# Graph transformer on one core: a chunk's first row gather waits for the landing of the chunk before

## The chip, the cores and the metric

One core of one Trainium2 chip runs the whole program. The metric is device time in microseconds (us) of one execution, from the first to the last instruction; lower is better. Time before: median 3657.33 us of 3 runs (3653.97 to 3659.31).

The engines are TensorE (PE; its weight load is PEld), VectorE (DVE), ScalarE (ACT), GpSimd (POOL) and SyncE (SP). Each has its own instruction queue and works through it in order. They tell each other by semaphores: an instruction or a DMA adds to one when it is done, another engine waits until it has reached a number.

## The reference, cut to what matters

Two layers of graph attention over N = 6250 nodes with D = 128 features, H = 8 heads, and E = 200000 directed edges that come sorted by their target (`dst`), then a feed-forward part for each node and a last layer norm:

```
loops = jnp.arange(n); src = concatenate([edge_index[0], loops]); dst = concatenate([edge_index[1], loops])
for l in range(L):                                   # L = 2
    xn = _layernorm(x, ln1_g[l], ln1_b[l])
    xp = xn + xn @ Wpos[l] + bpos[l] + deg[:, None] * Wdeg[l][0] + bdeg[l]
    q, k, v = (xp @ W[l] + b[l]).reshape(n, H, HD)   # one for each of Wq, Wk, Wv
    att = clip(einsum('ehd,ehd->eh', q[dst], k[src]) / scale, -50, 50)
    alpha = softmax of att over the edges of one dst
    aggr = segment_sum(v[src] * alpha[:, :, None], dst)
    x = x + (aggr @ Wo[l] + bo[l])
    x = x + gelu(_layernorm(x, ln2_g[l], ln2_b[l]) @ W1[l] + b1[l]) @ W2[l] + b2[l]
```

The expensive part is `k[src]` and `v[src]`: for each edge, one row of 256 f32 (1 KiB) out of a table in HBM, at a place that the data decide.

## The kernel before, in words

**Tables.** Before each layer the kernel has written `kv_table[l]` (a row of keys and values for each node) and `q_table[l]` to HBM. For layer 1 the node steps of layer 0 write them, tile by tile of 128 nodes (L780, L781).

**Units.** The edges of a layer are worked off in units. Most are *chunks* of CH = 1024 edges (T = 8 tiles of P = 128 edges). The edges of the last 8 (layer 0) or 10 (layer 1) node tiles are done as *blocks* instead: they are sorted by source on the chip, whole stretches of `kv_table` are loaded by SP (L729), and TensorE picks the rows by one-hot matmuls (L952) that ACT copies out (L1238). `Layer.unit_order` mixes the two: 165 chunks and 56 blocks in layer 0, 157 chunks and 70 blocks in layer 1, so 322 chunks and 126 blocks in all.

**What a chunk goes through.** POOL gathers its rows (`gather`, L1961): eight indirect DMAs, one for each tile of 128 edges, each moving 128 rows of 1 KiB into the chunk's buffer. TensorE spreads the queries to the edges (`spread_chunk`, L993), DVE multiplies them with the gathered keys (`make_products`, L1676, which waits at L1671 until all eight gathers have landed) and reduces them to scores (L1685), ACT makes the exponentials (L1260), DVE multiplies them with the gathered values (`make_messages`, L1700, which adds 1 to `msg_ready`), TensorE sums over the edges of a node (L1009), DVE adds that to the running sums (L1726). The steps for whole nodes (projection, feed-forward, next layer's tables) are put between the units by a table of slots.

**Buffers and semaphores of the gathers.** The gathered rows have a ring of RING_KV = 4 buffers, `kv[m % 4]`: three in the tile `kv_ring`, the fourth in the tile `arena`. Each buffer has a semaphore `gathered[m % 4]`, to which each of the chunk's eight gathers adds 16 when its rows have landed, 128 for a chunk. POOL's queue in this stage (`pool_edges`, L1975) holds nothing but the gathers of all chunks in order. The first gather of chunk m waits until `msg_ready` says that chunk m - 4 has been read out of the same buffer (L1963, L1964); chunk m = 3 waits for tables of the setup instead (L1965 to L1969); the first chunk of each layer waits for the layer's `kv_table` (L1978). POOL does not wait for its own gathers to land.

The seven lines that matter, of `gather`:

```
m = chunk(l, c)
if m >= RING_KV:
    e.wait_ge(msg_ready, chunk_unit(m - RING_KV) + 1)
...
for t in range(T):
    e.indirect_dma_start(kv[m % RING_KV][:, t, :], None, kv_table[l],
                         bass.IndirectOffsetOnAxis(ap=src_idx[:, c * T + t:c * T + t + 1], axis=0)
                         ).then_inc(gathered[m % RING_KV], 16)
```

Of the kernel before, what the change touches and what calls it, by code (L numbers as in the profile page):

```python
# [30 lines left out]
T = 8  # L31
# [21 lines left out]
RING_KV = 4  # L53
# [237 lines left out]
def graph_transformer(nc, x, src, dst, Wq, bq, Wk, bk, Wv, bv, Wo, bo, Wpos, bpos, Wdeg, bdeg,  # L291
                      ln1_g, ln1_b, ln2_g, ln2_b, W1, b1, W2, b2, out):
    with ExitStack() as ctx:
# [3 lines left out]
        def semaphore(name):  # L297
            return ctx.enter_context(nc.semaphore(name))
# [227 lines left out]
        gathered = [semaphore(f"gathered{i}") for i in range(RING_KV)]  # L526
# [80 lines left out]
        def chunk(l, c):  # L607
            return LAYERS[l].chunk0 + c
# [9 lines left out]
        def chunk_unit(m):  # L618

            l = max(l for l in range(L) if LAYERS[l].chunk0 <= m)  # L620
            return unit(l, LAYERS[l].chunk_at[m - LAYERS[l].chunk0])
# [74 lines left out]
        def wait_tables(e, l, of):  # L696

            if l == 0:
                for queue in range(2):
                    e.wait_ge(tables_out[2 * of + queue], 16 * len([g for g in groups if g[0] % 2 == queue]))  # L700
            else:
                for s in range(WORK):
                    e.wait_ge((kv_out, q_out)[of][s], 16 * layer_uses(s))
# [1256 lines left out]

        def gather(e, l, c):  # L1961
            m = chunk(l, c)
            if m >= RING_KV:  # L1963
                e.wait_ge(msg_ready, chunk_unit(m - RING_KV) + 1)  # L1964
            elif m == RING_KV - 1:  # L1965

                wait_tables(e, 0, 1)
                e.wait_ge(zero_out, 16 * L)
                e.wait_ge(win_out, 16)  # L1969
# [5 lines that stand above are left out]
        def pool_edges(e):  # L1975
            e.wait_ge(idx_ready, 4)
            for l in range(L):
                wait_tables(e, l, 0)  # L1978
                for c in range(LAYERS[l].ca):
                    gather(e, l, c)  # L1980
# [206 lines left out]
```

## Time and profile before

| what | value |
|---|---|
| median of 3 runs | 3657.33 us (3653.97 to 3659.31) |
| span of the profiled execution | 5559.9 us |
| POOL busy | 2472.4 us, 44% of that span |
| DVE busy | 2916.7 us, 52% |
| PE busy | 3461.6 us, 62% |
| ACT busy | 1771.1 us, 32% |
| DMA | 548.28 MB, mean 99 GB/s; of this 337.81 MB by POOL's gathers |

The profiled execution took 5559.9 us, which is 1.52 times the median of the runs that were timed: with the profiler recording, this program runs much longer. Durations of instructions come from that execution; its idle times belong to it alone. Busy time counts an engine's instructions; its waits, and the instructions with which it issues DMAs, are not in it, but a gather on POOL shows as an instruction of its own (DMA_INDIRECT), which ends before its data have moved.

### The profile page before, as it was taken

To read this page: it belongs to the slowest core of one execution; us is meant where nothing else is said; L and a number is where in the kernel's file an instruction comes from. 1 tells how busy PE (TensorE), PEld (TensorE's weight loads), DVE (VectorE), ACT (ScalarE), POOL (GpSimd) and SP (SyncE) were. 2 spreads that over 40 slices of the span, in tenths; PEclk is the share of its full clock that TensorE was granted. 3 is DMA by queue.
4 is the path that set the end of the run, shared out by engine and by line. 5 is a ranking of instruction groups with operands and counts; after the bars stand their busy time and mean duration, and the time that the engine had idled before them with its cause. 6 is when DMAs were issued, how large, how long until landed. Compare 5 with 4: busy or idle time off the path is not lost.

```text
span 5559.9 us, 72300 instructions
## 1 busy us (share of the span) xinstructions
PE 3461.6 (62%) x24196; PEld 2666.6 (48%) x24475; DVE 2916.7 (52%) x6780; ACT 1771.1 (32%) x4391; POOL 2472.4 (44%) x2597
## 2 busy tenths in 40 slices
PE   5834656655665656666566376666666566666666
PEld 4623445444454445444444254455555455545545
DVE  9944545554454545555455354554554454545455
ACT  2301232323333332323234133333333333333334
POOL 1065444444444444444542544445444454444443
PEclk7756777777777777777777677777777777777777
DMA  2133333333333333333332333333333333333332
GB/s 73 49 111 87 88 106 93 102 88 95 102 94 99 94 102 89 104 95 96 107 105 65 106 103 109 108 107 113 96 108 106 108 110 113 111 102 115 109 104 73
DMA packets 404556, 548.28 MB, mean 99 GB/s; under 512 B 78348, under 2 KB 318656, under 8 KB 403988
## 3 DMA queue, kind: packets, MB, share of 16 engines
q0 software_dynamic: 123648, 337.81, 20.9%
q1 hardware_dynamic: 273030, 198.56, 11.9%
q10 hardware_dynamic: 7506, 7.20, 0.4%
q8 instruction: 203, 3.33, 0.2%
q14 instruction: 169, 1.38, 0.1%
HBM read 518.00 MB, written 25.29 MB: 98 GB/s over the span
## 4 chain that ended last, share of the span: by engine, by line
PE 32%; another core or an unknown queue 30%; DVE 14%; issue 12%; ACT 10%; DVEq 0%; SPq 0%; DMA 0%; ACTq 0%
PE psum L952 7%; PE psum L993 4%; PE psum L1009 3%; ACT scratch L1227 3%; PE psum L1042 3%; PE psum L1026 3%; DVE att L1685 2%; PE psum L970 2%; ACT arena L1238 2%; DVE scratch L1676 2%; DVE kv_ring L1394 1%; PE psum L1123 1%; DVE work L1377 1%; DVE scratch L1700 1%
## 5 line engine op out<-in xcount | busy, mean ns | idle before, releaser
L1971 POOL DMA_INDIRECT kv_ring<-kv_table,src_idx x1936 | 1846.4, 954 | 2132.8 <-DVE scratch L1700 1501.1
L1227 ACT ACTIVATE scratch<-psum 128x512 f32<-128x512 f32 x1148 | 649.5, 570 | 2061.3 <-remote 1442.0
L952 PE MATMUL psum<-arena 128*128 128x256 f32 x1764 | 631.5, 486 | 464.2 <-issue 194.2
L1971 POOL DMA_INDIRECT arena<-kv_table,src_idx x640 | 607.8, 950 | 664.6 <-DVE scratch L1700 489.7
L1726 DVE SCALAR_TENSOR_TENSOR arena<-psum,in_block,arena 128x136 f32 x644 | 200.9, 353 | 1286.4 <-remote 1187.3
L993 PE MATMUL psum<-q_win,scratch 64*128 64x128 f32 x5152 | 534.3, 349 | 285.7 <-issue 149.9
L952 PEld LDWEIGHTS psum<-arena 128*128 128x128 f32 x1764 | 372.6, 236 | 621.0 <-issue 319.2
L1009 PE MATMUL psum<-scratch 128*64 128x136 f32 x5152 | 519.1, 330 | 185.4 <-issue 154.2
L993 PEld LDWEIGHTS psum<-q_win,scratch 64*128 64x128 f32 x5152 | 443.2, 243 | 343.1 <-issue 332.5
L1238 ACT COPY arena<-psum 128x512 f32<-128x512 f32 x504 | 265.1, 532 | 986.9 <-remote 524.7
L1685 DVE TENSOR_REDUCE att<-scratch 128x64 f32<-128x1024 f32 (+1 forms) x448 | 525.1, 1172 | 0.1
L1676 DVE TENSOR_TENSOR scratch<-psum,arena 128x512 f32<-128x512 f32 (+1 forms) x412 | 255.4, 646 | 507.4 <-remote 397.5
L1009 PEld LDWEIGHTS psum<-scratch 128*64 128x64 f32 x5152 | 376.8, 161 | 268.6 <-issue 245.6
L1676 DVE TENSOR_TENSOR scratch<-psum,kv_ring 128x512 f32<-128x512 f32 x484 | 313.7, 684 | 264.5 <-remote 182.6
L1026 PE MATMUL psum<-q_win,scratch 128*128 128x128 f32 x1764 | 272.1, 318 | 288.4 <-ACT arena L1238 270.5
L1042 PE MATMUL psum<-scratch 128*128 128x136 f32 x1764 | 309.2, 332 | 3.8 <-ACT work L1326 3.8
L1700 DVE TENSOR_TENSOR scratch<-kv_ring,psum 128x1024 f32<-128x1024 f32 x242 | 292.3, 1208 | 29.4 <-ACT psum L1260 24.2
L1042 PEld LDWEIGHTS psum<-scratch 128*128 128x128 f32 x1764 | 289.6, 238 | 8.6 <-issue 4.5
L1026 PEld LDWEIGHTS psum<-q_win,scratch 128*128 128x128 f32 x1764 | 273.4, 234 | 12.7 <-issue 3.9
L962 PEld LDWEIGHTS psum<-plan_mem,places 128*128 128x128 bf16 x322 | 35.9, 112 | 423.5 <-issue 372.6
L1700 DVE TENSOR_TENSOR scratch<-arena,psum 128x896 f32<-128x896 f32 (+1 forms) x206 | 232.1, 1127 | 9.0 <-ACT psum L1260 7.4
L1731 DVE TENSOR_TENSOR arena<-arena,psum 128x136 f32<-128x136 f32 x108 | 31.9, 295 | 330.6 <-PE psum L1042 200.0
(251 smaller groups left out, 4873.9 us busy)
## 6 DMA issues: line engine op xcount, KB each, us to landing
arena<-kv_table SPq DMA_DIRECT2D x126, 896.0 KB
kv_ring<-kv_table,src_idx POOLq DMA_INDIRECT x1936
q_win<-q_table SPq DMA_DIRECT2D x644, 32.0 KB
work<-kv_table SPq DMA_DIRECT2D x98, 128.0 KB
arena<-kv_table,src_idx POOLq DMA_INDIRECT x640
q_win<-q_table SPq DMA_DIRECT2D x126, 64.0 KB
work<-q_table SPq DMA_DIRECT2D x98, 64.0 KB
kv_table<-work SPq DMA_DIRECT2D x49, 128.0 KB
```

Of the source, the lines that this page charges most:

```text
L952: mm = e.matmul(to[:, t % 2 * 2 * D:(t % 2 + 1) * 2 * D], hot_source[:, t * P:(t + 1) * P], source_rows[:, t, :], start=True, stop=True)
L993: m = e.matmul(q_edge[h][:, t * P:(t + 1) * P], hotT[n % 2][h * HALF:(h + 1) * HALF, t * P:(t + 1) * P], q_win[h * HALF:(h + 1) * HALF, n ...
L1009: m = e.matmul(to[h * HALF:(h + 1) * HALF], by_edge[:, t * P + h * HALF:t * P + (h + 1) * HALF], msg[n % 2][:, h * T // 2 + t, :], start=t ...
L1026: m = e.matmul(q_edge[f % 2][:, (t - ts[0]) * P:(t - ts[0] + 1) * P], hotT[n % 2][:, t * P:(t + 1) * P], q_win[:, n % 2, :], start=True, s ...
L1042: m = e.matmul(edge_sum(l, u), hot[n % 2][:, t, :], msg[n % 2][:, t, :], start=t == 0, stop=t == last)
L1227: e.activation(to[:, at:at + width], apart[k % 2][:, 0:width], ACT.Relu, bias=1.0, scale=-1.0).then_inc(apart_read, 1)
L1238: e.copy(kv_block[:, ts[0]:ts[-1] + 1, :].rearrange("p t d -> p (t d)"), apart[k % 2][:, 0:len(ts) * 2 * D]).then_inc(apart_read, 1)
L1676: e.tensor_tensor(prod[:, ts[0] * P:(ts[-1] + 1) * P].rearrange("p (t d) -> p t d", d=D), q_edge[f % 2][:, 0:len(ts) * P].rearrange("p (t ...
L1685: e.tensor_reduce(raw_att.rearrange("p t h -> p (t h)"), prod[:, 0:ts * P].rearrange("p (g d) -> p g d", d=HD), AX_X, ALU.add).then_inc(sc ...
L1700: e.tensor_tensor(msg[n % 2][:, 0:ts, 0:D].rearrange("p t (h d) -> p t h d", d=HD), values.rearrange("p t (h d) -> p t h d", d=HD), ex[:, ...
L1726: e.scalar_tensor_tensor(out=row, in0=of_edges, scalar=in_block[:, k, i:i + 1], in1=row, op0=ALU.mult, op1=ALU.add).then_inc(acc_added, 1)
L1971: e.indirect_dma_start(kv[m % RING_KV][:, t, :], None, kv_table[l], bass.IndirectOffsetOnAxis(ap=src_idx[:, c * T + t:c * T + t + 1], axis ...
```

## The change

Before the first gather of each chunk but the very first, POOL waits until the eight gathers of the chunk before have landed in full: until `gathered` of that chunk's buffer has reached 128 times the number of times that the buffer has been filled. The wait stands ahead of the one for `msg_ready`. Nothing else is changed.

```
         def gather(e, l, c):
             m = chunk(l, c)
+            if m >= 1:
+                e.wait_ge(gathered[(m - 1) % RING_KV], 16 * T * ((m - 1) // RING_KV + 1))
             if m >= RING_KV:
                 e.wait_ge(msg_ready, chunk_unit(m - RING_KV) + 1)
             elif m == RING_KV - 1:
```

## Rows read from the trace of the kernel before

**Rows 1.** The page: the span, and each engine's busy time, share and instructions.

```profile
span 5559.9 us, 72300 instructions
PE 3461.6 (62%) x24196; PEld 2666.6 (48%) x24475; DVE 2916.7 (52%) x6780; ACT 1771.1 (32%) x4391; POOL 2472.4 (44%) x2597
```

**Rows 2.** Windows: setup, gathers of layer 0, gathers of layer 1, the end.

```profile
core 0: us, PE busy (x) PEld busy (x) DVE busy (x) ACT busy (x) POOL busy (x), PEclk, DMA share, GB/s
0.00:278.00 278.00, 199.68 (x2136) 152.45 (x2136) 255.89 (x445) 75.85 (x160) 18.15 (x21) 0.75 0.20 61
278.00:3053.00 2775.00, 1647.39 (x11152) 1269.17 (x11286) 1403.84 (x3326) 827.90 (x2080) 1265.14 (x1320) 0.73 0.33 96
3053.00:5503.00 2450.00, 1578.78 (x10678) 1216.53 (x10823) 1223.83 (x2902) 839.72 (x2087) 1189.12 (x1256) 0.76 0.36 108
```

**Rows 3.** Groups of POOL's gathers, by buffer: count, busy us, mean ns of one.

```profile
L1971 POOL DMA_INDIRECT kv_ring<-kv_table,src_idx x1936 | 1846.4, 954 | 2132.8 <-DVE scratch L1700 1501.1 <-issue 534.0 <-DMA kv_table<-work 70.3
L1971 POOL DMA_INDIRECT arena<-kv_table,src_idx x640 | 607.8, 950 | 664.6 <-DVE scratch L1700 489.7 <-issue 174.9
```

**Rows 4.** POOL's waits: us in total, times, longest us.

```profile
POOL kv_ring L1971 <- DVE scratch L1700: 1501.1, 198, 17.9
POOL kv_ring L1971 <- issue: 534.0, 1736, 1.2
POOL arena L1971 <- DVE scratch L1700: 489.7, 66, 20.5
POOL arena L1971 <- issue: 174.9, 574, 0.3
POOL kv_ring L1971 <- DMA kv_table<-work: 70.3, 1, 70.3
```

**Rows 5.** Timeline of POOL: two chunks' gathers without a wait, then a waiting one.

```profile
2012.76 0.94 POOL L1971 DMA_INDIRECT kv_ring<-kv_table,src_idx  x1 [14.54 <-DVE scratch L1700]
2014.01 0.94 POOL L1971 DMA_INDIRECT kv_ring<-kv_table,src_idx  x1 [0.30 <-issue]
...
2031.51 0.95 POOL L1971 DMA_INDIRECT kv_ring<-kv_table,src_idx  x1 [0.30 <-issue]
2042.85 0.94 POOL L1971 DMA_INDIRECT arena<-kv_table,src_idx  x1 [10.39 <-DVE scratch L1700]
```

**Rows 6.** Timeline of POOL: the first and the last gather of the program.

```profile
278.64 9.23 POOL L1971 DMA_INDIRECT kv_ring<-kv_table,src_idx  x1 [27.59 <-DMA kv_table<-scratch]
...
5501.81 0.95 POOL L1971 DMA_INDIRECT kv_ring<-kv_table,src_idx  x1 [0.30 <-issue]
```

**Rows 7.** Timeline where layer 1 begins: its first chunk's gathers, queries and product.

```profile
3053.18 0.94 POOL L1971 DMA_INDIRECT kv_ring<-kv_table,src_idx  x1 [70.25 <-DMA kv_table<-work]
...
3057.65 2.08 PE L993 MATMUL psum<-q_win,scratch 64*128 64x128 f32 x16 [3.53 <-issue]
...
3061.93 0.95 POOL L1971 DMA_INDIRECT kv_ring<-kv_table,src_idx  x1 [0.30 <-issue]
...
3064.83 1.29 DVE L1676 TENSOR_TENSOR scratch<-psum,kv_ring 128x512 f32<-128x512 f32 x2 [14.30 <-issue]
```

**Rows 8.** The gathers' line: who waited for it (us, times).

```profile
  DVE scratch L1676: 14.3, 1
```

**Rows 9.** Windows behind the gather of 2031.51; the last two columns are DMA.

```profile
2033.00:2033.50 0.50, 0.00 (x0) 0.00 (x0) 0.00 (x0) 0.00 (x0) 0.00 (x0) 0.50 0.67 156
2033.50:2034.00 0.50, 0.00 (x0) 0.00 (x0) 0.00 (x0) 0.00 (x0) 0.00 (x0) 0.50 0.28 107
2034.00:2034.50 0.50, 0.00 (x0) 0.00 (x0) 0.00 (x0) 0.00 (x0) 0.00 (x0) 0.50 0.00 0
```

**Rows 10.** DMA issues of other queues, KB each, median us to landing.

```profile
q_table<-scratch SPq DMA_DIRECT2D x1, 384.0 KB, 2.8
q_table<-arena SPq DMA_DIRECT2D x3, 384.0 KB, 3.3
kv_table<-arena SPq DMA_DIRECT2D x3, 768.0 KB, 3.9
```

More of the change, by code:

```diff
@@ L1962, in gather @@
             m = chunk(l, c)
+            if m >= 1:
+                e.wait_ge(gathered[(m - 1) % RING_KV], 16 * T * ((m - 1) // RING_KV + 1))
             if m >= RING_KV:
```

## The prediction

> **What bounds the kernel now.** The first thing to read is the span against the times. The profiled execution took 5559.9 us [rows 1], the timed runs 3657.3 us in the median. So 1902.6 us of what the profile shows as idle do not exist in the timed runs, and a share of the span (POOL 44%) says little about them. The idle times of this profile can't be used as slack. What can be used is work: an engine whose work, laid end to end, comes near to 3657 us has no slack in the timed runs, whatever the profile shows around it.
>
> So I next read the engines' work per stage [rows 2]. From 278 to 5503 us PE is busy 1647.4 + 1578.8 = 3226.2 us, DVE 2627.7 us, ACT 1667.6 us, POOL 2454.2 us. With the 278.6 us before the first gather and the 57.1 us behind the last one (which ends at 5501.81 + 0.95 = 5502.76, [rows 6]; 5559.9 - 5502.8) PE would come to 3561.9 us, and that at a granted clock of 0.73 to 0.76, with more to gain where it is higher. DVE comes to 2963.4 us.
>
> POOL's busy time leaves something out. In the timeline of POOL [rows 5] a gather lasts 0.94 to 0.95 us, but the next one begins 1.25 us after its begin: from 2012.76 to 2031.51 there are 15 steps of 1.25 us with 0.30 us between two gathers, and nothing ends that gap but the queue's own issue. The waits [rows 4] show the total: 1736 + 574 = 2310 such gaps, 534.0 + 174.9 = 708.9 us. The other 264 gathers were held by `msg_ready`. Had they not been, each would still have had its 0.30 us, 79.2 us. POOL's path is then, with the busy time of [rows 3]:
>
> 278.6 (before the first gather) + 2454.2 (1846.4 + 607.8, 2576 gathers) + 708.9 + 79.2 + 70.3 (the wait for layer 1's table, [rows 4]) + 57.1 (after the last gather) = 3648.3 us.
>
> That is 99.8% of the median of 3657.3 us. I read it so: in the timed runs POOL issues gathers nearly without pause, and the ring of four buffers is mostly waiting to be filled. In the profiled execution it is the other way round: there POOL waits 1501.1 + 489.7 = 1990.8 us for DVE to free a buffer [rows 4].
>
> A page of the Trainium skill bears on the choice of 1.25 over 0.95 us. "Perfetto Trace Analysis", section "Per-instruction lifecycle: what the profiler-reported window actually captures", says of GpSimd that the reported span of an instruction is unreliable and that one should take the spacing from start to start. By the durations alone POOL's path would be 2454.2 + 406.0 = 2860.2 us and far from the bound. By the spacing it is the bound. The equal steps in [rows 5] agree with the page.
>
> **The change part by part.** It adds one wait ahead of each chunk but the first, 321 of 322. It removes and moves nothing. Behind the waiting gather in POOL's queue stand only the gathers of this and the later chunks; SP's queue, with the loads of queries, plans and source rows, is not touched. Who waits for POOL is DVE, at L1671.
>
> What one wait costs. Up to now the first gather of a chunk could start 0.30 us after the last one of the chunk before. Now it starts when that one has landed. The profile lists no landing for POOL's gathers, but it has one place where something waited for them alone: the begin of layer 1 [rows 7]. The eighth gather of the first chunk begins at 3061.93 and ends at 3062.88; the queries had been spread by 3059.73; DVE's product begins at 3064.83, and the line's own view names it as the one that waited for a gather [rows 8]. From the end of the last gather to the start of the waiting engine: 1.95 us, and 2.90 us from its begin. In place of 0.30 us this costs 1.65 us for a chunk.
>
> Bounds for that. Below: behind the gather that begins at 2031.51 and ends at 2032.46 the DMA engines still move 107 GB/s until 2034.00 and nothing after it [rows 9], so its data were through after at most 1.54 us; with no time for the signal that is 1.54 - 0.30 = 1.24 us. Above: transfers of other queues take 2.8 to 3.9 us from issue to landing [rows 10]; 3.9 us from the begin is 2.95 us from the end, less 0.30 is 2.65 us. 2.90 us lies near the 2.8 and 3.3 us of the 384 KB transfers, so I keep 1.65 us, and take 3.3 us (2.05 us for a chunk) as the upper end that is still likely, since the timed runs move the same bytes in two thirds of the time.
>
> The skill has a price too: "DMA: Bandwidth & Descriptors", section "Anatomy of one DMA — SWDGE (gpsimd) path", gives about 2.0 us plus bytes over 436e3 for one DMA, for 128 KiB 2.30 us. Taken from the begin of the gather, this would be 1.05 us for a chunk, an estimate from that page of 336 us in all and 3984 us. The row's 2.90 us is a measurement of these very gathers, and the sum goes by it.
>
> How many count. Of 321 waits one falls on the first chunk of layer 1, inside the 70.3 us for which POOL stands anyway; the rows before it landed long ago. 320 are left, all on POOL's path: 320 x 1.65 = 528 us. What hides nothing: after the change POOL's path is 3648.3 + 528 = 4176 us, above PE's 3561.9 us by 614 us. The 9 us by which the median lies over the old path are covered by it. The very first chunk has no wait, and the start of DVE hangs on it alone, so nothing is added there.
>
> Against the profiled execution's own time the same edit would look small: there 264 of 322 chunk starts waited for DVE [rows 4], 7.5 us in the mean (1990.8 / 264), long after the rows had landed. At most the other 56 or so would pay 1.65 us, 92 us on 5559.9 us, most of it taken up by the ring. I therefore expect a profiled span near 5560 to 5650 us, and a far greater change in the timed runs.
>
> **The rivals.**
>
> Hidden (3657 us). The profiler itself lengthens the 0.30 us gap, and in the timed runs the step from gather to gather is shorter. A chunk on POOL then takes 7 steps p, plus 2.90 us: the change is free if 7p + 2.90 is at most (3657.3 - 406.0) / 322 = 10.10 us, that is p at most 1.03 us. For it: the profile is 1.52 times as long as the runs, so the recording does cost something, and PE at 3561.9 us is a second engine that could be the bound. Against it: the step is 1.25 us in quiet and in busy stretches alike, and POOL has few instructions.
>
> Partly hidden (about 3910 us). The step lies between: with p = 1.14 us a chunk takes 10.88 us, 406.0 + 322 x 10.88 = 3909 us; with p = 1.10 us 3819 us.
>
> Landing slower (up to 4500 us). With 2.65 us for a chunk it is 3648.3 + 848 = 4496 us. DMA is shared with source loads of 896 KB, but its mean share is only 0.33 to 0.36 [rows 2].
>
> Faster (3605 us). If POOL had slack of 1.65 us or more in a chunk (p at most 1.03 us), the wait would only thin out the bursts of gathers, and SP's loads for the blocks would meet fewer packets of theirs. Its place is the block units; the price is the difference of the two landings above, 1.95 - 1.54 = 0.41 us, for 126 blocks: 52 us, which gives 3605 us. It can decide only under the same condition as the hidden case, and only if PE waits for such loads.
>
> That the wait does nothing because the semaphore is already there is the hidden case; it does name the right buffer and the full count.
>
> **How the numbers follow.** POOL's path plus the landing, 4176 us: chance 0.71; its own range by the landing is 3648.3 + 320 x 1.24 = 4045 us to 3648.3 + 320 x 2.05 = 4304 us. Partly hidden: 0.11. Hidden: 0.11. Slower landing: 0.04. Faster: 0.03. The range takes the first case and the partly hidden one from p = 1.10 us on: 3820 to 4300 us, which leaves out some 0.2. A difference of 0.2%, 7 us, is about what can be told from no change here. Faster 0.03, within it 0.11, slower 0.86.
>
> **What would show it.** In the profile after: the first gather of a chunk that follows at once on another shows an idle time of about 1.95 us instead of 0.30 us, with no gap under 1.7 us between chunks; steps inside a chunk stay at 1.25 us; 264 or fewer waits for DVE remain. The profiled span hardly grows while the timed median grows by 14%. If the median stays, POOL's step in the timed runs is shorter than in the trace, and the first part of my reading is wrong. If it grows by much more than 650 us, the landing is slower under the denser traffic of the timed runs.

## The result

The changed kernel took 4328.1 us in the median (4324.4 to 4337.0), the kernel before 3657.3 us: ratio 1.185, 95% interval 1.183 to 1.187, or 671 us more. The forecast was 4176 us (519 us more), range 3820 to 4300 us. The direction and the mechanism held; the size was missed by 152 us, and the time lies 28 us outside the range.

The profiled execution of the changed kernel took 4323.2 us, like its timed runs. That was the first surprise: the one of before took 5559.9 us [rows 1] against 3657 us timed. The kernel before was therefore profiled once more (the run `before_again`, below), and this time it took 3645.9 us, like its timed runs. It is this second profile that the changed kernel can be compared with. What the first one showed is told further down.

The heads of the two pages, the kernel before (second profile) first, the changed one behind it (engine: busy us, share of the span, instructions):

```profile
span 3645.9 us, 72300 instructions
PE 2879.4 (79%) x24196; PEld 2282.0 (63%) x24475; DVE 2897.0 (79%) x6780; ACT 1761.8 (48%) x4391; POOL 2485.1 (68%) x2597
```

```profile
span 4323.2 us, 72896 instructions
PE 3167.7 (73%) x24475; PEld 2447.6 (57%) x24475; DVE 2895.4 (67%) x6780; ACT 1763.6 (41%) x4391; POOL 2484.8 (57%) x2597
```

The same window in both, engines and columns as in [rows 2], before first:

```profile
600.00:2800.00 2200.00, 1797.06 (x14692) 1423.90 (x14875) 1763.02 (x4228) 1117.06 (x2809) 1615.80 (x1691) 0.91 0.53 159
```

```profile
600.00:2800.00 2200.00, 1646.02 (x12262) 1266.99 (x12263) 1465.48 (x3504) 912.54 (x2296) 1341.40 (x1401) 0.84 0.44 131
```

POOL issued 1691 gathers in these 2200 us and issues 1401 after the change; PE has 14692 matmuls and then 12262. Nothing got slower on DVE, ACT or POOL (their busy times are equal); less of everything fits into the same time. PE's busy time rose from 2879.4 to 3167.7 us with the granted clock down from 0.91 to 0.84 in this window, but PE is not what the kernel waits for.

POOL's waits tell where the time is. The kernel before, second profile (us in total, times, longest us):

```profile
POOL kv_ring L1971 <- issue: 584.0, 1916, 0.5
POOL arena L1971 <- issue: 193.2, 634, 0.3
POOL kv_ring L1971 <- DMA kv_table<-work: 44.4, 1, 44.4
POOL kv_ring L1971 <- DVE scratch L1700: 27.3, 18, 6.2
POOL arena L1971 <- DVE scratch L1700: 4.9, 6, 2.3
```

The changed kernel:

```profile
POOL kv_ring L1973 <- issue: 519.6, 1693, 0.5
POOL kv_ring L1973 <- DMA kv_ring<-kv_table,src_idx: 394.5, 160, 4.4
POOL kv_ring L1973 <- DMA arena<-kv_table,src_idx: 207.2, 80, 4.9
POOL arena L1973 <- DMA kv_ring<-kv_table,src_idx: 187.1, 79, 4.5
POOL arena L1973 <- issue: 170.6, 560, 0.3
POOL kv_ring L1973 <- DMA kv_table<-work: 49.1, 1, 49.1
```

These answer to [rows 4]. Before, only 24 gathers were held by DVE, 32.2 us in all, and 2550 followed at once. After, 319 chunk starts wait for the landing of the rows before them: 394.5 + 207.2 + 187.1 = 788.8 us, 2.47 us each. That replaces 2550 - 2253 = 297 gaps (777.2 - 690.2 = 87.0 us) and 28.4 us of waiting for DVE: 788.8 - 87.0 - 28.4 = 673.4 us. The wait for layer 1's table adds 4.7 us. Together 678 us of a difference of 677.3 us between the two spans. The whole change is on POOL's path, and nothing gives any of it back.

Two chunk starts in the timeline of POOL after the change, to be read against [rows 5]:

```profile
1514.75 0.94 POOL L1973 DMA_INDIRECT kv_ring<-kv_table,src_idx  x1 [3.14 <-DMA arena<-kv_table,src_idx]
...
1526.77 0.94 POOL L1973 DMA_INDIRECT kv_ring<-kv_table,src_idx  x1 [2.04 <-DMA kv_ring<-kv_table,src_idx]
```

The landing takes 2.04 us of POOL's idle time in one case and 3.14 us in the other. The forecast had one number for all, 1.95 us. Over all 319 waits the shortest is 1.97 us, the median 2.12 us and the longest 4.93 us: 193 take at most 2.2 us (2.08 us in the mean) and 126 take more (3.08 us in the mean). So most landings are near the forecast, and a long tail lifts the mean to 2.47 us. The other signs that the prediction named are there: no gap between chunks that waits for a landing is under 1.7 us, 2112 of 2254 steps inside chunks are still 1.25 us, and 2 waits for DVE are left.

POOL's path was the bound before and is the bound now; DVE shows how much further ahead it lies. DVE waited for gathered rows of the three buffers in `kv_ring` 66 times in the kernel before, and does so 191 times now (the second profile of before, then the changed kernel):

```profile
DVE scratch L1676 <- DMA kv_ring<-kv_table,src_idx: 179.3, 66, 14.5
```

```profile
DVE scratch L1676 <- DMA kv_ring<-kv_table,src_idx: 842.7, 191, 14.5
```

### The profile page after: what moved, and what is told of

Its sections match the earlier page's. It is cut to its first block, busy times and chain, and to the rows that moved or that the text cites. A ratio compares the mean times of both kernels' runs of the same rounds, so it can differ in the third digit from the quotient of the medians.

```text
span 4323.2 us, 72896 instructions
## 1 busy us (share of the span) xinstructions
PE 3167.7 (73%) x24475; PEld 2447.6 (57%) x24475; DVE 2895.4 (67%) x6780; ACT 1763.6 (41%) x4391; POOL 2484.8 (57%) x2597
## 4 chain that ended last, share of the span: by engine, by line
POOL 56%; issue 33%; DVE 5%; PE 3%; DMA 3%; ACT 0%; POOLq 0%; DVEq 0%; SPq 0%
POOL kv_ring L1973 42%; POOL arena L1973 14%; DMA kv_ring<-kv_table,src_idx 2%; DVE kv_ring L1394 2%; PE psum L828 1%; DVE kv_ring L1397 1%; PE psum L853 1%; DVE arena L1654 0%; DMA scratch<-in_src 0%; DVE arena L1377 0%; PE psum L1123 0%; DVE scratch L1602 0%; DVE scratch L1377 0%; DVE work L1377 0%; DVE arena L1408 0%
## 5 line engine op out<-in xcount | busy, mean ns | idle before, releaser
L1973 POOL DMA_INDIRECT arena<-kv_table,src_idx x640 | 611.1, 955 | 361.1 <-DMA kv_ring<-kv_table,src_idx 187.1
L993 PE MATMUL psum<-q_win,scratch 64*128 64x128 f32 x5152 | 484.2, 341 | 342.3 <-DVE scratch L1676 267.5
L952 PE MATMUL psum<-arena 128*128 128x256 f32 x1764 | 540.9, 432 | 62.5 <-ACT arena L1238 59.3
L1009 PE MATMUL psum<-scratch 128*64 128x136 f32 x5152 | 436.7, 320 | 53.2 <-DVE work L1871 20.4
L952 PEld LDWEIGHTS psum<-arena 128*128 128x128 f32 x1764 | 332.2, 210 | 185.7 <-ACT arena L1238 123.3
L1009 PEld LDWEIGHTS psum<-scratch 128*64 128x64 f32 x5152 | 345.9, 157 | 96.8 <-issue 69.5
L1260 ACT ACTIVATE psum<-att 128x64 f32<-128x64 f32 (+1 forms) x448 | 101.5, 227 | 716.7 <-DVE att L1691 707.2
L1026 PEld LDWEIGHTS psum<-q_win,scratch 128*128 128x128 f32 x1764 | 233.7, 209 | 103.2 <-issue 98.7
L1042 PE MATMUL psum<-scratch 128*128 128x136 f32 x1764 | 270.9, 303 | 9.2 <-ACT work L1326 4.7
L1042 PEld LDWEIGHTS psum<-scratch 128*128 128x128 f32 x1764 | 250.9, 210 | 14.5 <-issue 10.4
L1227 ACT ACTIVATE arena<-psum 128x512 f32<-128x512 f32 x252 | 135.1, 536 | 218.6 <-PE psum L940 218.6
```

The lines of the kernel that those rows point to most:

```text
L952: mm = e.matmul(to[:, t % 2 * 2 * D:(t % 2 + 1) * 2 * D], hot_source[:, t * P:(t + 1) * P], source_rows[:, t, :], start=True, stop=True)
L993: m = e.matmul(q_edge[h][:, t * P:(t + 1) * P], hotT[n % 2][h * HALF:(h + 1) * HALF, t * P:(t + 1) * P], q_win[h * HALF:(h + 1) * HALF, n ...
L1009: m = e.matmul(to[h * HALF:(h + 1) * HALF], by_edge[:, t * P + h * HALF:t * P + (h + 1) * HALF], msg[n % 2][:, h * T // 2 + t, :], start=t ...
L1026: m = e.matmul(q_edge[f % 2][:, (t - ts[0]) * P:(t - ts[0] + 1) * P], hotT[n % 2][:, t * P:(t + 1) * P], q_win[:, n % 2, :], start=True, s ...
L1042: m = e.matmul(edge_sum(l, u), hot[n % 2][:, t, :], msg[n % 2][:, t, :], start=t == 0, stop=t == last)
L1227: e.activation(to[:, at:at + width], apart[k % 2][:, 0:width], ACT.Relu, bias=1.0, scale=-1.0).then_inc(apart_read, 1)
```

## The experiments

All times are medians; each kernel ran beside runs of the kernel before on the same chip, and is compared with those. Where a variant is set against the changed kernel, which ran elsewhere, it is by what each takes more than the kernel before beside it: 671 us for the changed kernel.

### Is the long profile a matter of recording?

`before_again`: the kernel before, unchanged.

> The kernel before, unchanged, to see whether its profiled execution is stretched each time. In the first one the span was 5559.9 us against 3657 us timed; that of the changed kernel was 4323.2 us against 4328 us, not stretched at all. If the stretching belongs to one unlucky recording, the span is now near 3655 us and POOL's rows show it without pause: some 56 or more chunk starts with 0.30 us before them become some 300, and the waits for DVE shrink from 1990.8 us to under 60 us. If it belongs to this kernel whenever it is recorded, the span is again above 5000 us and what POOL does in the timed runs stays inferred.

Measured: span 3645.9 us, timed 3647.7 us (one run), beside 3650.9 us. So this recording cost nothing to speak of; the rows of the second profile stand above. POOL issues 2550 of 2576 gathers 0.30 us after the one before, as the forecast had inferred from the sum of work. Why the first profile was so long is taken up below, under "A second kind of chip".

### What is the price, and is it the landing?

`wait_two_back`: the same wait for the chunk before the last.

```
-            if m >= 1:
-                e.wait_ge(gathered[(m - 1) % RING_KV], 16 * T * ((m - 1) // RING_KV + 1))
+            if m >= 2:
+                e.wait_ge(gathered[(m - 2) % RING_KV], 16 * T * ((m - 2) // RING_KV + 1))
```

> The same wait, but for the chunk before the last one: chunk m waits until the rows of chunk m - 2 have landed. The number of waits and of rows in flight at a wait is nearly that of the change; only the landing on POOL's path is gone, since a whole chunk's gathers (10 us) lie between. Theory: the price of the change is the landing alone: 3657 us, at most some us more for 320 waits that are already met. Rival (the wait itself, or POOL's stop, has a price of its own): above 3700 us.

Measured 3654.4 us beside 3646.7 us, ratio 1.0016 (1.0004 to 1.0028), so 1 to 10 us more. POOL's waits in it:

```profile
POOL kv_ring L1973 <- issue: 577.7, 1880, 1.9
POOL arena L1973 <- issue: 191.2, 626, 0.5
POOL kv_ring L1973 <- DMA kv_table<-work: 47.5, 1, 47.5
POOL kv_ring L1973 <- DVE scratch L1700: 35.4, 54, 4.6
POOL arena L1973 <- DVE scratch L1700: 4.3, 14, 0.3
```

The 2574 gaps between gathers, those held by DVE included, sum to 808.6 us here and to 809.4 us in the kernel before (584.0 + 193.2 + 27.3 + 4.9). So waits that are already met cost nothing that shows between the gathers; in this profile the few us more lie at the start (the first gather ends 3.5 us later) and in the wait for layer 1's table (3.1 us more). The price of the change is not that of a wait instruction.

`wait_gather1` and `wait_gather2`: the change's wait moved behind the chunk's first gather, or behind its second.

```
             for t in range(T):
+                if t == 1 and m >= 1:    # t == 2 in the other
+                    e.wait_ge(gathered[(m - 1) % RING_KV], 16 * T * ((m - 1) // RING_KV + 1))
                 e.indirect_dma_start(kv[m % RING_KV][:, t, :], None, kv_table[l],
```

> The added wait is moved behind the first gather of a chunk: it stands ahead of the second one. One gather (1.25 us) now covers part of the landing. Theory (the change costs the landing of the last gather on POOL's path, and this landing differs from chunk to chunk): in the profile of the changed kernel POOL idles 2.0 to 4.1 us ahead of a chunk, 2.47 us in the mean; what is left of each after 0.30 and 1.25 us sums to about 296 us: 3953 us. Rival 1 (each landing takes the same 2.1 us): 0.55 us for a chunk, 176 us: 3833 us. Rival 2 (what costs is that POOL stops and starts again, not how long the rows take): as the change, near 4328 us.

> The added wait stands ahead of the third gather of a chunk: two gathers (2.50 us) cover the landing. Theory: only the landings above 2.8 us are left, summed over the profile of the changed kernel about 57 us: 3714 us. Rival 1 (all landings take 2.1 us): nothing left, 3657 us. Rival 2 (stopping and starting costs): near 4328 us.

Measured 3995.4 us (ratio 1.095, 1.092 to 1.098) and 3735.5 us (1.025, 1.022 to 1.029), beside 3650.9 us: 345 and 85 us more, where the theory had 296 and 57, equal landings 176 and 0, and a price for stopping as such 670 and 670. The two rivals are out. One gather of 1.25 us ahead of the wait takes off about half of the 671 us, two take off seven eighths, and what is left with two can only come from landings that are much longer than 2.1 us. The waits of `wait_gather1` that the profile puts down to the landing:

```profile
POOL kv_ring L1973 <- DMA kv_ring<-kv_table,src_idx: 176.6, 134, 4.0
POOL kv_ring L1973 <- DMA arena<-kv_table,src_idx: 113.1, 80, 4.2
POOL arena L1973 <- DMA kv_ring<-kv_table,src_idx: 101.6, 80, 3.7
```

They are 391.3 us in 294 waits. Ahead of 26 more second gathers POOL pauses for 68.1 us in all, which the profile calls "issue" but which stand at the same place; with them it is 459.4 us in 320, 1.44 us each. 2.47 less 1.25 us would be 1.22 us: with the next gather already on its way the landing is a little longer still.

### What makes some landings long?

`after_small_src` and `before_small_src`: the changed kernel and the kernel before, with the source load of each block but the first cut to its first tile. The block edges are then summed from wrong rows.

```
-            e.dma_start(source_rows, kv_table[l][TB * o * P:TB * (o + 1) * P, :].rearrange("(t p) d -> p t d", p=P)
+            n = TB if m == 0 else 1
+            e.dma_start(source_rows[:, 0:n], kv_table[l][TB * o * P:(TB * o + n) * P, :].rearrange("(t p) d -> p t d", p=P)
```

> The changed kernel with the source load of each block (SP, 896 KB) cut to its first 128 KB after the first one; the other rows of that buffer are then left from the first load, so that the sums of the block edges are of wrong rows. All instructions of the engines are as before. Theory (the landings above 2.2 us, some 128 of 320, are those that meet a source load, and there are 126 blocks): the mean idle time ahead of a chunk falls from 2.47 us to about 2.1 us, 120 us in all: 4208 us. Rival (the long landings come from the gathers' own traffic or from the other small loads): 4328 us.

> The kernel before with the source load of each block cut from 896 KB to its first 128 KB after the first one; the sums of the block edges are then of wrong rows. Theory (before the change POOL issues gathers without pause and nobody waits on its path for a landing): the loads are free, 3657 us within 7 us. Rival (the loads slow the gathers' descriptors or TensorE's blocks, which share the bound): 3600 us or less.

Measured: 4245.9 us beside 3650.9 us, 595 us more where the changed kernel has 671: the cut takes off 76 us, where the theory had 120 and the rival 0. On the kernel before the same cut does nothing: 3648.0 beside 3646.7 us, ratio 1.000 (0.999 to 1.001). The landing waits of `after_small_src`:

```profile
POOL kv_ring L1974 <- DMA kv_ring<-kv_table,src_idx: 358.4, 160, 4.7
POOL arena L1974 <- DMA kv_ring<-kv_table,src_idx: 177.8, 80, 3.4
POOL kv_ring L1974 <- DMA arena<-kv_table,src_idx: 173.7, 78, 4.1
```

709.9 us in 318 waits, 2.23 us each, against 2.47 us: 79 us less in sum, which is the 76 us of the timed runs. The many short landings stay as they were (2.07 us in the mean of those up to 2.2 us); those above fall from 126 with 3.08 us in the mean to 104 with 2.56 us. What was cut of SP's 896 KB loads makes up that much of the long landings; it is on POOL's path only because of the change. Waits up to 4.7 us remain; what lengthens these, the rest of the loads or other transfers, was not tried.

### How far above the others was POOL's path?

`before_seven` and `after_seven`: seven gathers for a chunk instead of eight from the fifth chunk on, in the kernel before and in the changed one; an eighth of the chunk edges is summed from wrong rows.

```
-            for t in range(T):
+            for t in range(T if m < RING_KV else T - 1):
```

(The counts of the waits for `gathered` are lowered to match.)

> The kernel before with seven gathers for a chunk instead of eight, from the fifth chunk on; the eighth tile's rows are then left from an earlier chunk, so that an eighth of the chunk edges is summed from wrong rows. Theory (POOL's path is the bound, 1.25 us for a gather): 318 gathers less take 318 x 1.25 = 397 us off, 3260 us, or less than that off if another engine is the bound by then: PE's work and the ends come to 3562 us at the clock of the stretched profile and to less at a higher one. So 3260 to 3560 us, and the difference from 3657 us tells how much below POOL the next bound lies. Rival (POOL is not the bound): 3657 us.

> The changed kernel with seven gathers for a chunk instead of eight, from the fifth chunk on; an eighth of the chunk edges is then summed from wrong rows. Theory (POOL's path with the landing is the bound of the changed kernel by more than 600 us): the full 318 x 1.25 = 397 us come off, 3931 us. Rival (the landing wait has made TensorE or DVE the bound, for example by a lower clock): less than 300 us come off, above 4030 us.

Measured: 3545.7 us for the first, 101 us less than the 3646.7 us beside it (ratio 0.971, 0.970 to 0.973), and 3969.2 us for the second, 322 us more than the kernel before beside it instead of 671 us: 348 us less. In the kernel before, some 397 us of POOL's work went (318 gathers of 1.25 us), and after 101 us of it another bound took over: its POOL now waits for DVE,

```profile
POOL kv_ring L1971 <- DVE scratch L1700: 262.9, 78, 11.1
POOL arena L1971 <- DVE scratch L1700: 86.6, 34, 11.1
```

349.5 us instead of 32.2 us. So POOL's path was the bound, with some 100 us between it and the next one. In the changed kernel most of the 397 us comes off. What is missing is in the landing waits of `after_seven`:

```profile
POOL kv_ring L1973 <- DMA kv_ring<-kv_table,src_idx: 420.7, 160, 5.5
POOL arena L1973 <- DMA kv_ring<-kv_table,src_idx: 208.8, 79, 6.0
POOL kv_ring L1973 <- DMA arena<-kv_table,src_idx: 206.1, 80, 5.2
```

835.6 us, 47 us more than the changed kernel's 788.8 us, and 397 - 47 = 350 us. That each landing meets more of the other traffic, with less time between chunks, would explain the 47 us; it was not tested.

### A second kind of chip

The runs so far, but for the first profile, took 3647 to 3657 us for the kernel before; the two of these chips that the record numbers are 12 and 14. The runs that follow fell on chips 0, 5 and 15, on which every run of it took 5441 to 5561 us, half as long again. No chip was seen in both conditions, but each was used at one time only: "kind of chip" is a name for the two conditions, and that they belong to the chip is not shown. The kernel before was timed there and not profiled; the profile of `more_blocks`, which is nearly the same kernel, looks like [rows 1] and [rows 4]: a span of 5421.2 us, a mean granted clock of 0.758, and POOL held by DVE 269 times for 1887.8 us. The first profile of before (5559.9 us, clock 0.744; 0.888 in the second one) was in all likelihood taken in this condition; its chip is not on record.

`after_half_rows`, run three times (`half_rows_2`, `half_rows_3`): the changed kernel with gathers of half rows, 512 bytes, from the fifth chunk on, all sums of wrong rows.

```
-                e.indirect_dma_start(kv[m % RING_KV][:, t, :], None, kv_table[l],
+                w, rows = (2 * D, kv_table[l]) if m < RING_KV else (D, kv_table[l].rearrange("n (two d) -> (n two) d", two=2))
+                e.indirect_dma_start(kv[m % RING_KV][:, t, 0:w], None, rows,
```

> The changed kernel whose gathers move rows of 512 bytes instead of 1 KiB from the fifth chunk on (the keys' half, out of a view of the same table with half rows); the number of gathers, of rows and of waits is unchanged, and the sums are of wrong rows. It tells how much of the landing depends on the bytes. Theory (most of the 2.1 us between the last gather's end and the next chunk is the fixed way to the signal; only collisions with other transfers depend on traffic): the steady idle ahead of a chunk stays near 2.0 us, the long ones get rarer, 4328 us falls by 30 to 130 us, to 4200 to 4300 us, and the step from gather to gather stays 1.25 us. Rival (the rows' own time on the DMA engines is what POOL waits for): the idle is about halved, 1.0 us less for each of 320 chunks: 4000 us or less.

> The changed kernel with gathers of 512-byte rows from the fifth chunk on (sums of wrong rows), again, since the first time it fell where the kernel before took 5486 us and POOL was not the bound. Beside a before of 3650 us: theory (the steady part of the landing is a fixed way to the signal; the first run had 224 us for 113 landings, 1.98 us each) 4200 to 4300 us; rival (the rows' time on the DMA engines) 4000 us or less. Beside a before of 5486 us: as the first time, 5240 us.

> The changed kernel with gathers of 512-byte rows from the fifth chunk on (sums of wrong rows). Beside a before of 3650 us: theory (the steady part of the landing is a fixed way to the signal) 4200 to 4300 us, rival (the rows' time on the DMA engines) 4000 us or less. Beside a before of 5500 us: 5240 to 5350 us as on the other two chips.

`after_again`: the changed kernel itself.

> The changed kernel, unchanged, on whatever chip this falls, since two conditions have shown: the kernel before took 3647 to 3657 us in some runs and 5486 us in the last ones, where POOL waited for DVE in two thirds of the chunk starts. Theory (the landing costs what POOL has no slack for): beside a before of 3650 us it is again 4328 us, ratio 1.18; beside a before of 5486 us POOL has 6 us of slack in the mean chunk and the ratio is 1.00 to 1.02, at most 5580 us. Rival (the wait costs 2.1 us for each chunk wherever it stands): 5486 + 670 = 6156 us there, ratio 1.12.

`two_back_2`: `wait_two_back` again.

> The wait for the chunk before the last one, again. On chips where the kernel before takes 3650 us it cost 6 us. On two chips where the kernel before took 5486 and 5550 us, the change made it 4.8% faster (5279 against 5550 us), which neither of my theories had. If what helps there is that fewer gathers are in flight or queued at once, this wait does little, since a chunk's gathers are in flight as before: within 1% of 5500 us. If what helps is the pause of 2 us between chunks' gathers, in which other transfers get through, it does nothing either. If it helps as much as the change, the bound on how far POOL runs ahead of the landing is what counts. Beside a before of 3650 us: 3654 us again.

`more_blocks` (three times) and `more_blocks_both` (twice): the kernel before with more of layer 0's node tiles done as blocks.

```
-NBS = 8, 10
+NBS = 9, 10     # more_blocks_both: 10, 10
```

> The kernel before with 9 instead of 8 node tiles of layer 0 done as blocks: 4 chunks less for POOL, 7 blocks more for SP, TensorE, ACT and DVE. Theory (POOL's path of gathers is the bound and the next bound lies about 100 us below it, as seven gathers for a chunk showed): 4 x 8 x 1.25 = 40 us off POOL's path, less what the 7 more units cost where DVE already waits: 3605 to 3635 us. Rival (the other engines are as near to the bound as POOL): 3650 us or slower.

> The kernel before with 9 instead of 8 node tiles of layer 0 done as blocks, again. Beside a before of 5486 us it took 5427 us. Beside a before of 3650 us: 4 chunks less on POOL's path, 3605 to 3635 us; rival (the other engines are as near to the bound) 3650 us or more.

> The kernel before with 9 instead of 8 node tiles of layer 0 done as blocks. Beside a before of 5500 us it was 1% faster twice. Beside a before of 3650 us: POOL's path is 40 us shorter, 3605 to 3635 us; rival (the other engines are as near to the bound) 3650 us or more.

> The kernel before with 10 instead of 8 node tiles of layer 0 done as blocks: 8 chunks less for POOL (80 us), 14 blocks more for the others. Theory: POOL's path falls to about 3570 us, but with seven gathers for a chunk the next bound showed at 3546 us, and 14 more units of some 7 us of DVE and TensorE each move that up to about 3600 us or above: 3590 to 3640 us. Rival (balance was already best at 8): above 3650 us.

> The kernel before with 10 instead of 8 node tiles of layer 0 done as blocks, again. Beside a before of 5486 us it took 5353 us. Beside a before of 3650 us: 3590 to 3640 us; rival (balance was already best at 8): above 3650 us.

Measured on these chips:

| kernel | us | before, same chip | ratio (95% interval) |
|---|---|---|---|
| after_again | 5278.8 | 5550.5 | 0.952 (0.949 to 0.955) |
| after_half_rows | 5240.3 | 5485.6 | 0.955 (0.953 to 0.957) |
| half_rows_2 | 5348.4 | 5550.5 | 0.964 (0.962 to 0.966) |
| half_rows_3 | 5244.9 | 5488.0 | 0.959 (0.954 to 0.964) |
| two_back_2 | 5535.1 | 5488.0 | 1.012 (1.007 to 1.018) |
| more_blocks | 5426.9 | 5485.6 | 0.989 (0.986 to 0.991) |
| more_blocks_2 | 5489.9 | 5550.5 | 0.990 (0.987 to 0.994) |
| more_blocks_3 | 5423.3 | 5488.0 | 0.990 (0.987 to 0.992) |
| more_blocks_both | 5353.2 | 5485.6 | 0.974 (0.972 to 0.977) |
| more_blocks_both_2 | 5432.9 | 5550.5 | 0.979 (0.975 to 0.983) |

The change that costs 18.5% on one kind of chip makes the kernel 4.8% faster on the other (one chip, four runs; the three runs with half rows, on three chips, go the same way). Both theories of `after_again` are wrong there, one with 1.00 to 1.02, the other with 1.12. The wait for two chunks back, which was expected to do nothing, costs 1.2% there. Its profile shows that the price is indeed mostly gone; POOL's waits in it:

```profile
POOL kv_ring L1973 <- DVE scratch L1700: 1113.6, 173, 14.7
POOL arena L1973 <- DVE scratch L1700: 275.4, 47, 11.5
POOL kv_ring L1973 <- DMA kv_ring<-kv_table,src_idx: 121.9, 56, 4.8
POOL arena L1973 <- DMA kv_ring<-kv_table,src_idx: 82.0, 35, 4.3
POOL kv_ring L1973 <- DMA arena<-kv_table,src_idx: 50.0, 23, 3.5
```

Only 114 of 321 chunk starts wait for a landing, 253.9 us, and 220 wait for DVE, 1389.0 us where it was 1990.8 us [rows 4]: the buffers come free sooner. The gain is on the other side, in what waits for TensorE's results. DVE's wait for the edge sums, which TensorE makes, is listed as "remote", because the signal comes long after the recorded matmul; in the first profile of before, in `two_back_2` and in `after_again`:

```profile
DVE arena L1726 <- remote: 1187.3, 149, 19.0
```

```profile
DVE arena L1726 <- remote: 1097.3, 148, 19.9
```

```profile
DVE arena L1726 <- remote: 730.0, 164, 8.3
```

The longest waits are cut by more than half with the change and not at all with the wait for two chunks back: 45 of these waits are longer than 8.4 us in the first (681.8 us), 45 in the second (665.8 us) and none in the third. What the change takes away there are two chunks' gathers issued back to back: it leaves at most 8 gathers in a row, where the first profile of before has 39 rows of exactly 16 and `two_back_2` has 40. That fits the stretch in which [rows 5] and [rows 9] lie. POOL issues 16 gathers from 2012.76 us on, and in the window of the first profile that follows, columns as in [rows 2], POOL alone works for 8 us:

```profile
2027.50:2035.50 8.00, 0.00 (x0) 0.00 (x0) 0.00 (x0) 0.00 (x0) 3.79 (x4) 0.50 0.31 90
```

The traces say more when all such stretches are counted, those of 3 us and more between the first and the last gather in which neither TensorE nor DVE nor ACT has an instruction. The first profile of before has 99, the longest of 15.9 us. All begin within 1.4 us of a gather's begin, though only 63% of the time lies there. Gathers whose begins are at most 1.4 us apart are called a row here: 75 of the stretches end behind such a row, 2.1 us after its last gather in the median, about a landing later. `two_back_2` has 92, the longest of 15.4 us; `after_again` has 65, and none is over 6.8 us, as a row there ends after 8 gathers. So in this condition the standstills go with gathers in a row and mostly end when these have landed. It is not the gathers alone: the second profile of before, with rows of up to 773 gathers, has 5 such stretches, the longest of 4.6 us. No run changed the gathers' rows by anything but the waits, so that they bring on the standstills is likely and not shown; what stands still in TensorE, and why in one condition only, stays open. It is not a matter of bytes: with half of them and the same waits the ratios are 0.955 to 0.964, no better than 0.952.

The landings with half rows are 102.4 + 75.6 + 46.1 = 224.1 us for 113 waits in the first of the three,

```profile
POOL kv_ring L1974 <- DMA kv_ring<-kv_table,src_idx: 102.4, 53, 3.4
POOL arena L1974 <- DMA kv_ring<-kv_table,src_idx: 75.6, 37, 4.3
POOL kv_ring L1974 <- DMA arena<-kv_table,src_idx: 46.1, 23, 4.7
```

1.98 us each, and 182.2 / 88 = 2.07 us and 192.0 / 96 = 2.00 us in the second and third, against 253.9 / 114 = 2.23 us with whole rows (`after_again`, on the chip of the second). The medians, which the few long ones do not move, are 1.86, 1.85 and 1.84 us against 2.08 us. Half the bytes take off 0.23 us, and with 512-byte rows some 1.85 us are left. These are only the chunk starts that DVE did not hold. On the other kind of chip this could not be measured.

More blocks beat the kernel before on these chips by 1% and by 2.1 to 2.6%. Whether they do where POOL's path is the bound, for which `before_seven` speaks, stays untested; all five runs fell on the second kind of chip.

## Why the prediction was right or wrong

- **The first step, what the profile is.** The text ahead of the prediction says that the program runs longer because the profiler records, and the prediction speaks of idle time that does not exist in the timed runs. The cause was wrong: a recording in the first condition cost nothing (a span of 3645.9 us, timed 3647.7 us), and the first profile looks like one of the second condition. What was concluded held all the same, since it rested on work and not on idle time: POOL's path, 3648.3 us by the rows, is 3645.9 us in the proper profile, with first gather 280.4, busy 2467.1, gaps 777.2, DVE 32.2, table 44.4 and end 44.8 us. That the two agree so closely is in part luck: table and end were 38 us shorter, busy time, gaps and DVE together 34 us longer.
- **POOL as the bound, with a step of 1.25 us.** Right. 2550 gaps of 0.30 us stand in the proper profile, `before_seven` gets faster, and the path leads the next bound by 100 us; which engine bounds `before_seven` was not looked into. The spacing was the right measure, not the duration.
- **320 waits, all on the path, nothing behind them that hides.** Right: 319 in the profile, and the sum of them accounts for the difference of the spans.
- **1.65 us for a wait.** This is the term that was mis-sized. With 319 waits of 2.47 us, 2.17 us is what each adds over the 0.30 us. The number came from one landing, at the begin of layer 1, where DVE and not POOL waited and where the traffic was that of a start. The missing 0.52 us are of two sorts. The 193 short landings take 2.08 us instead of 1.95, which is 0.13 us for each; why, is not separated. The 126 long ones add 0.39 us in the mean over all, and 0.24 us of this goes with the cut of SP's source loads (`after_small_src`); the rest stays open. One landing was taken for the mean of 320. The prediction had named the denser traffic as what could lengthen the landing, and then gave this only the step from 1.65 to 2.05 us in the range; 2.17 us is just beyond.
- **Terms that made up for it.** The landings alone were 165 us longer than forecast, 319 x (2.47 - 1.95). The table's wait and the end were 21.2 and 12.8 us shorter than in the first profile, and the gathers' busy time and the start 12 and 2 us longer. So some 20 us of the miss were made up for by luck.
- **The estimate from the Trainium skill** ("DMA: Bandwidth & Descriptors", section "Anatomy of one DMA — SWDGE (gpsimd) path"), 2.30 us from the begin of the gather, is too low here: 0.95 + 2.47 = 3.4 us in the mean, and 0.95 + 1.97 = 2.9 us in the shortest. The measurement decides.
- **Hidden and partly hidden.** Wrong for the chips that were timed. On the second kind POOL has the slack, and the price is mostly hidden there, but not by the condition that these rivals gave: the step is still 1.25 us and not 1.03 us, and the slack comes from the others' standing still. The outcome there is that of the rival which the prediction gave 0.03, faster, though by 272 us and not by 52. Part of its mechanism may hold, shorter bursts of gathers; for its place nothing speaks: no profile here puts a wait down to SP's source loads, and the gain is in the waits for TensorE.
- **The profiled span "hardly grows", to 5560 to 5650 us.** Wrong in both conditions: the span is 4323.2 us where before it is 3645.9 us, and 5239.0 us where before it is 5559.9 us. The forecast took the first profile's idle times for a matter of recording, and left out that the wait could shorten the standstills.

## What to carry to other kernels

When an engine's gathers laid end to end give the timed median, it is most likely the bound, whatever its busy share says, and a wait for its own DMAs then costs the full way of the last one to the signal, every time. Take that price from the mean of many landings under load, not from one. Put such a wait two gathers later, or one chunk further back: 85 us and under 10 us here, instead of 671 us. And when the span of the profile and the timed runs differ by half, find out first whether both come from the same conditions, since a change can have the opposite sign in the two.

## What the runs showed of the hardware that was not expected

- Two conditions: the same kernel takes 3647 to 3657 us on some chips and 5486 to 5550 us on others. DVE, ACT and POOL are busy for the same time within 1% (2897.0 and 2916.7, 1761.8 and 1771.1, 2485.1 and 2472.4 us in the two profiles of before), TensorE for 2879.4 and 3461.6 us at a granted clock of 0.888 and 0.744, and in the longer one DVE waits up to 19.0 us at a time for TensorE's edge sums.
- A gather of 128 rows is issued every 1.25 us whether the rows are 512 bytes or 1 KiB.
- From the end of a gather's issue to the engine that waits for its rows it takes 2.0 to 4.9 us under load, 2.47 us in the mean, 2.12 us in the median (`after`). With half the bytes the median goes from 2.08 to 1.85 us (in the second condition).
- In the second condition the stretches in which TensorE, DVE and ACT all stand still lie in rows of gathers and mostly end some 2 us after the last one. The change, which ends each row after 8 gathers, made the kernel 4.8% faster there; that the shorter rows are the cause is likely and not shown.
